# Reordered slots, a straight expert stage, and the Newton rounds of the rotary scale on POOL

## What is computed

```python
x = layernorm(x + ssm(x))              # state space layer, 64 states
x = layernorm(x + moe(x))              # three routed linears, 8 experts, top 2
x = layernorm(x + ssm2(x))             # second state space layer, 16 states
x = layernorm(x + transformer(x))      # 6 layers
```

```python
def attn_layer(x, Wqkv, qs, ks, Wo):       # 16 heads of 64
    q, k, v = split(x @ Wqkv)
    q, k = l2norm(q) * qs, l2norm(k) * ks
    q, k = rotary(q), rotary(k)            # cos and sin tables with a scale
    # queries in windows of 32 see their own and the previous window of keys, masked
    return softmax(8 * q @ k.T) @ v @ Wo

x = attn_layer(shift_tokens(x), ...) + x
x = (a * gelu(gate)) @ W2 + b2 + x         # a, gate = layernorm(shift_tokens(x)) @ W1 + b1
```

## Time and profile before

| | |
|---|---|
| median of 3 runs | 5227.65 us (5224.09 to 5231.3) |
| profiled execution | 5220.35 us |
| its span, first to last instruction | 5218.5 us |
| mean granted PE clock over the span | 0.924 |
| expert stage | 126 to 1033 us |
| transformer, its 96 full passes | some 1240 to 5100 us |

### The profile page before, as it was taken

How to read it: one execution, slowest core, us unless ns; L and a number is a source line. 1 busy time by engine, 2 the same in 40 slices (tenths; PEclk the granted TensorE clock), 3 DMA queues, 4 the chain that set the end, 5 groups by cost and what they waited for, 6 DMA issues and landing times.

```text
span 5218.5 us, 147460 instructions
## 1 busy us (share of the span) xinstructions
PE 4516.0 (87%) x64229; PEld 3255.0 (62%) x64613; DVE 3483.4 (67%) x7580; ACT 2311.9 (44%) x4138; POOL 2147.3 (41%) x1332
## 2 busy tenths in 40 slices
PE   4999899885888888888888888888888888888887
PEld 3666666563666666666666666666666666666665
DVE  5434343435777777777777777777777777778884
ACT  2111111122555555555555555555555555555553
POOL 0000000003555555555555555555555555555552
PEclk7999999997999999999999989999999999999997
DMA  1000000001111111111111111111111111111110
GB/s 70 1 1 0 0 0 0 9 1 43 29 33 30 33 41 39 33 31 32 41 39 33 33 29 44 40 33 30 36 43 38 30 30 33 45 39 32 32 33 24
DMA packets 70585, 152.25 MB, mean 29 GB/s; under 512 B 14523, under 2 KB 43078, under 8 KB 69574
## 3 DMA queue, kind: packets, MB, share of 16 engines
q1 hardware_dynamic: 69958, 143.09, 9.4%
HBM read 27.69 MB, written 2.10 MB: 6 GB/s over the span
## 4 chain that ended last, share of the span: by engine, by line
PE 44%; DVE 22%; ACT 5%; issue 5%; POOL 0%; DMA 0%; SPq 0%; DVEq 0%; POOLq 0%; ACTq 0%
PE pQ L1480 8%; PE pS L1464 7%; PE pO L1524 6%; PE pC L1580 5%; PE pO L1511 4%; ACT sq L1355 4%; PE pM L1546 4%; PE pM L1535 3%; PE pT L1511 3%; DVE E L1196 3%; DVE mx L1194 2%; DVE rot L1216 2%; DVE m L1220 2%; DVE ve L1254 2%; DVE n L1231 2%
## 5 line engine op out<-in xcount | busy, mean ns | idle before, releaser
L1138 POOL TENSOR_TENSOR rot<-rot,m 128x1024 f32<-128x1024 f32 x384 | 905.1, 2357 | 602.8 <-DVE m L1220 602.8
L1130 POOL TENSOR_TENSOR rot<-rot,rn 128x1024 f32<-128x1024 f32 x384 | 731.9, 1906 | 281.1 <-DVE rn L102 281.1
L1147 POOL TENSOR_TENSOR E<-E,rc 128x512 f32<-128x512 f32 x384 | 400.5, 1043 | 943.1 <-DVE rc L1206 943.0
L1346 ACT ACTIVATE E<-E 128x512 f32<-128x512 f32 x384 | 241.7, 629 | 1091.5 <-DVE E L1196 1091.5
L1511 PE MATMUL pO<-PT,V 64*64 64x32 f32 x12288 | 482.5, 232 | 199.6 <-ACT PT L1362 199.6
L1194 DVE TENSOR_REDUCE mx<-pS 128x8 f32<-128x512 f32 x384 | 264.2, 688 | 548.6 <-PE pS L1464 548.4
L1511 PEld LDWEIGHTS pO<-PT,V 64*64 64x64 f32 x12288 | 440.9, 149 | 284.2 <-issue 284.2
L1464 PE MATMUL pS<-kT,qT 64*32 64x64 f32 x24576 | 493.1, 238 | 87.1 <-issue 57.3
L1464 PEld LDWEIGHTS pS<-kT,qT 64*32 64x32 f32 x24576 | 424.0, 120 | 172.2 <-issue 172.1
L1216 DVE TENSOR_TENSOR rot<-pQ,tabl 128x1024 f32<-128x1024 f32 x384 | 469.5, 1223 | 54.0 <-ACT sq L1355 52.0
L1511 PE MATMUL pT<-PT,V 64*64 64x32 f32 x12288 | 484.6, 233 | 0.0
(11 more groups left out here) (221 smaller groups left out, 7932.3 us busy)
## 6 DMA issues: line engine op xcount, KB each, us to landing
V<-V SPq DMA_DIRECT2D x192, 384.0 KB, 3.5
xs<-XT SPq DMA_DIRECT2D x192, 64.0 KB, 2.9
V<-V SPq DMA_DIRECT2D x96, 128.0 KB, 3.3
ys<-XT SPq DMA_DIRECT2D x192, 64.0 KB, 2.0
wq<-in_wqkv SPq DMA_DIRECT2D x6, 512.0 KB, 4.0
wk<-in_wqkv SPq DMA_DIRECT2D x6, 512.0 KB, 4.0
wv<-in_wqkv SPq DMA_DIRECT2D x6, 512.0 KB, 3.9
wo<-in_wo SPq DMA_DIRECT2D x6, 512.0 KB, 4.0
```

The source lines that it names most:

```text
L1130: e.tensor_tensor(r, r, rn[n % 2][:, u * HEADS:(u + 1) * HEADS].unsqueeze(2).to_broadcast([P, HEADS, HD]), ALU.mult)\
L1138: e.tensor_tensor(rot[j % RING][:, :], rot[j % RING][:, :], m2[:, :, :].rearrange("p h d -> p (h d)"), ALU.add)\
L1147: e.tensor_tensor(ev, ev, rc[:, g, :].unsqueeze(2).to_broadcast([P, NW, KEYS]), ALU.mult).then_inc(g_no.sem, 1)
```

## The change

In the expert stage the loop goes and so does b_xst with POOL's copy: all 17 passes are written out, and PE and DVE read X itself. In the transformer the three Newton rounds move to POOL, ahead of unit_scale(R, 0), as four operations each; clamp and seed stay on DVE. All engines' lists get a new order: probs(Dn, 3) moves ahead, values(R, 0) into slot 0, and turn(R, 0) to that slot's end; values(R, 1) into slot 2; back becomes back(C) in slot 0 of the next pass. On DVE, statistics comes after rotate 0 and hidden after less_max 3 and rotate 3; POOL runs root after the first rotary_add; SP fetches the shifted half of V after the weights of the feed-forward and before ys, and the third weight at the end of the pass.

```diff
+def pool_rsqrt(eng, st, n, step, y, h, t):
+    def own(k):
+        eng.wait_ge(st.sem, st.at(step, n, 4 * ROUNDS - k))
+    for r in range(ROUNDS):
+        if r:
+            own(4 * r)
+        eng.tensor_tensor(t, y, y, ALU.mult).then_inc(st.sem, 1)
+        own(1 + 4 * r)
+        eng.tensor_tensor(t, t, h, ALU.mult).then_inc(st.sem, 1)
+        own(2 + 4 * r)
+        eng.tensor_scalar(t, t, 1.0, 1.5, ALU.mult, ALU.add).then_inc(st.sem, 1)
+        own(3 + 4 * r)
+        eng.tensor_tensor(y, y, t, ALU.mult).then_inc(st.sem, 1)
...
         def passes(run, eng):
-            run((0, 0), None)
-            run((1, 1), (0, 0))
-            with eng.Fori(0, (NSEQ - 2) // 2) as i:
-                for p in range(2):
-                    n = 2 * i + (2 + p)
-                    run((n, p), (n - 1, 1 - p))
-            run(None, (NSEQ - 1, 1))
+            for n in range(NSEQ + 1):
+                run((n, n % 2) if n < NSEQ else None, (n - 1, (n - 1) % 2) if n else None)
...
-                        e.wait_ge(gr.sem, gr.at("st", n))
                         if later(n):
                             e.wait_ge(ar.sem, ar.at("ctc", n - 1))
                         for t in range(T):
-                            m = e.transpose(pm[0][:, t * P:(t + 1) * P], xst[p][:, t * P:(t + 1) * P], ident[:, :])
+                            m = e.transpose(pm[0][:, t * P:(t + 1) * P], X[:, n, t, :], ident[:, :])
...
@@ SP @@
-                if R and starts(R):
-                    e.wait_ge(p_v.sem, p_v.at("b", 2 * R - 1))
-                    e.dma_start(wqkv[2][:, :], I["wqkv"][R // NSEQ, :, 2 * N:3 * N]).then_inc(wqkv_l[2], 16)
...
+                if R is not None:
+                    v, w = V[R % 2][:, :, 0, :], V[R % 2][:, :, 1, :]
+                    e.wait_ge(a_v.sem, a_v.at("b", 2 * R))
+                    e.dma_start(w[WIN:P, 0, :], v[0:P - WIN, 0, :]).then_inc(vs_l[R % 2], 16)
+                    e.dma_start(w[0:WIN, 1, :], v[P - WIN:P, 0, :]).then_inc(vs_l[R % 2], 16)
                 if Dn is not None:
                     fetch_ys(Dn)
...
                     e.wait_ge(a_v.sem, a_v.at("b", 2 * R + 1))
                     e.dma_start(w[WIN:P, 1, :], v[0:P - WIN, 1, :]).then_inc(vs_l[R % 2], 16)
+                    if starts(R + 1) and R + 1 < NP:
+                        e.dma_start(wqkv[2][:, :], I["wqkv"][(R + 1) // NSEQ, :, 2 * N:3 * N]).then_inc(wqkv_l[2], 16)
@@ POOL @@
                 if u == 0:
-                    e.wait_ge(v_nt.sem, v_nt.at("rs", n))
+                    e.wait_ge(v_nt.sem, v_nt.at("sd", n))
+                    pool_rsqrt(e, g_nt, n, "rs", rn[n % 2][:, :], rh[:, :], rt[:, :])
+                    e.wait_ge(g_nt.sem, g_nt.at("rs", n))
...
-                unit_scale(R, 0)
-                root(C)
-                by_sum(B, 0)
-                rotary_add(A, 0)
-                last_root(F)
-                for k in range(1, 4):
+                for k in range(4):
                     unit_scale(R, k)
                     by_sum(B, k)
                     rotary_add(A, k)
+                    if k == 0:
+                        root(C)
+                    if k == 1:
+                        last_root(F)
@@ DVE, roots @@
-                vector_rsqrt(e, v_nt, n, "rs", rn[n % 2][:, :], n2[:, :], rh[:, :], rt[:, :])
+                y = rn[n % 2][:, :].bitcast(I32)
+                e.wait_ge(v_nt.sem, v_nt.at("mn", n))
+                e.tensor_scalar(y, n2[:, :].bitcast(I32), 1, None, ALU.logical_shift_right).then_inc(v_nt.sem, 1)
+                if n:
+                    e.wait_ge(g_nt.sem, g_nt.at("rs", n - 1))
+                e.tensor_scalar(rh[:, :], n2[:, :], -0.5, None, ALU.mult).then_inc(v_nt.sem, 1)
+                e.wait_ge(v_nt.sem, v_nt.at("sh", n))
+                e.tensor_scalar(y, y, -1.0, MAGIC, ALU.mult, ALU.add).then_inc(v_nt.sem, 1)
```

More of the change, by code:

```diff
@@ L451, in _ @@
                 e.dma_start(dst, src).then_inc(loaded, 16)
[L453 to L462, removed]
         @block.vector
@@ L581, in r_lg @@
                         e.wait_ge(ar.sem, ar.at("xT", n))
[L582 removed]
+                        if n >= 2:
                             e.wait_ge(vm.sem, vm.at("lc", n - 2))
@@ L1317, in _ @@
                 squares(A, 1)
-                last_normal(F)
+                last_stats(F)
                 less_max(B, 2)
-                hidden(C, 0)
                 sums(B, 2)
@@ L1323, in _ @@
                 squares(A, 2)
+                last_normal(F)
                 less_max(B, 3)
+                hidden(C, 0)
+                sums(B, 3)
+                rotate(A, 3)
                 hidden(C, 1)
                 hidden(C, 2)
-                sums(B, 3)
-                rotate(A, 3)
-                ffn_add(C)
                 squares(A, 3)
                 roots(A)
+                ffn_add(C)
         @block.scalar
@@ L1403, in _ @@
             for A, R, B, Dn, C, F in passes():
+                probs(Dn, 3)
                 exponent(B, 0)
                 square(A, 0)
-                probs(Dn, 3)
+                heads_out(Dn, 3)
+                values(R, 0)
                 turned(R, 0)
-                heads_out(Dn, 3)
-                affine(C)
                 exponent(B, 1)
                 square(A, 1)
+                affine(C)
+                probs(B, 0)
+                turned(R, 1)
+                heads_out(B, 0)
+                probs(B, 1)
+                exponent(B, 2)
+                square(A, 2)
                 gelu(C, 0)
                 gelu(C, 1)
-                probs(B, 0)
-                turned(R, 1)
+                heads_out(B, 1)
+                turned(R, 2)
                 gelu(C, 2)
-                heads_out(B, 0)
-                exponent(B, 2)
-                square(A, 2)
-                probs(B, 1)
-                turned(R, 2)
-                heads_out(B, 1)
-                values(R, 0)
+                values(R, 1)
+                probs(B, 2)
                 exponent(B, 3)
                 square(A, 3)
-                probs(B, 2)
+                heads_out(B, 2)
                 turned(R, 3)
-                heads_out(B, 2)
-                values(R, 1)
         @block.tensor
@@ L1604, in _ @@
                 scores(B, 0)
+                probs(Dn, 3)
                 project(A, 0)
-                probs(Dn, 3)
+                back(C)
+                attend(Dn, 3)
+                values(R, 0)
                 turn(R, 0)
-                last(F)
-                attend(Dn, 3)
-                normed(C)
                 scores(B, 1)
                 project(A, 1)
+                normed(C)
+                combine(Dn)
+                probs(B, 0)
+                turn(R, 1)
                 hidden(C, 0)
-                probs(B, 0)
-                combine(Dn)
-                turn(R, 1)
+                attend(B, 0)
+                last(F)
+                scores(B, 2)
+                probs(B, 1)
+                project(A, 2)
+                attend(B, 1)
+                turn(R, 2)
                 hidden(C, 1)
-                attend(B, 0)
-                scores(B, 2)
-                project(A, 2)
+                values(R, 1)
+                scores(B, 3)
+                probs(B, 2)
+                project(A, 3)
                 hidden(C, 2)
-                probs(B, 1)
-                turn(R, 2)
-                attend(B, 1)
-                values(R, 0)
-                scores(B, 3)
-                project(A, 3)
-                contract(C)
-                probs(B, 2)
-                turn(R, 3)
-                attend(B, 2)
-                values(R, 1)
-                back(Dn)
+                attend(B, 2)
+                turn(R, 3)
+                contract(C)
 def layout(i):
```

29 lines of the change are left out of this document (12 added, 17 removed).

## The result

The changed kernel takes 5077.88 us (median of 3, 5071.0 to 5081.36) against 5227.65: ratio 0.9711, interval [0.9689, 0.9733]. The profiled execution took 5071.0 us, with a span of 5069.2 us. The forecast was 5066.

The account below looks back on a forecast made before the run. PE was taken to bound both stages, so its rests and low clock counted. From the profiled 5220 us, 75 (expert stage) and 79 (transformer) came off, giving 5066; own range 5010 to 5130, 8-in-10 range 4940 to 5205.

Parts of the forecast that it names:

- Expert stage, 75 us: Expert stage: 53 us of PE's wait plus 31 of slow clock, less 9 staying; ends 53 and 84.
- Newton on POOL, 0.35 each: Transformer slot 0: 12 dependent POOL operations at 0.35 us each, 4.2 us a pass; ends 1.3 and 8.4.
- the pow row: POOL's pow on two columns, 0.70 us: upper end per Newton operation, and the argument against leaving out the fixed part.
- Full-clock pass of 38.8: Transformer: one new pass walked at full clock takes 38.8 us, against 38.49 before.
- the port rule: Slot 0: POOL can block DVE's tensor_scalar through shared ports; ve could wait for the add, pass 39.2 instead of 38.8.
- The three rests of the walk: PE's rests in a new transformer pass: 2.1 us before contract, 1.4 before hidden 1, 0.55 before normed.
- Low clock, 0.7 us a pass: Transformer: low clock in a third to half of passes, 1.5 to 2.5 us each, 0.7 on average, giving 39.5.
- Transformer, 79 us: Transformer: passes fall from 40.33 to 39.5 us, times 95, a gain of 79 us.
- Sum, 154 us: Whole kernel: 75 us from the expert stage and 79 from the transformer, off 5220, giving 5066 us.
- The clock did not stay low in every pass: Rival, transformer: clock stays low in every pass, 40.96 us each, 5205 us in all; chance 0.15.
- POOL's operations kept under the 0.48: Rival, slot 0: POOL's chain bounds, a loss above 0.48 us per operation; at 0.70, 5465 us; chance 0.09.
- straight code did not come late: Rival, expert stage: straight code comes late, gaining only the rest or nothing, 5090 to 5145 us; chance 0.04.

Follow-up runs that it names:

- The filler: Changed kernel plus one thrown-away 512-column matmul per expert-stage sequence, between its last transposes and the third router's small matmuls: 5046.7 us, ratio 0.9642.
- fourth round: Changed kernel with a fourth Newton round on POOL, 4 more dependent operations: 5160.09 us, ratio 0.9863.
- The first experiment: Kernel before with only the straight expert stage (no loop, no b_xst), transformer untouched: 5153.44 us, ratio 0.9848.

## Why the prediction was right

- *Expert stage, 75 us:* 68, and 73 by the averages of all profiles. The rest of 3.8 us went whole and nothing came in its place; straight code cost nothing visible. The low clock was mis-sized twice. I had taken the first pair of sequences for the pattern (4.4 us of low clock for two), while over the whole stage it was 3.0 a sequence; and 1.5 a sequence stayed, where I had 0.6, so that they are 52.05 apart and not 50.4 to 51.5. The filler shows what it hangs on: with the stretch of transposes and 8-column matmuls broken up, every sequence takes 50.55.
- *Newton on POOL, 0.35 each:* 0.38. The two shapes gave the fixed part and the slope rightly; the pow row was no guide. That nothing covers the chain was right for a full-clock pass (fourth round: +1.5), not for a slow one (+0.5), where PE comes late anyway.
- *Full-clock pass of 38.8:* 39.05. The Newton rounds are 0.3 longer by the rows and the wait at hidden 1 is 0.24 shorter; no run takes the quarter apart. It is not the port rule, for which the prediction had named 39.2: in these passes ve took 0.28 and was not held by the add; it was held in the slow passes, where PE came late. The three rests of the walk stand in the waits, contract and normed within 0.1 us.
- *Low clock, 0.7 us a pass:* 0.6, but as two thirds of the passes at 1.0, not a third to a half at 1.5 to 2.5. The product was nearer than its two factors, and that is luck.
- *Transformer, 79 us:* 69, from two slips that partly cancel. The walked pass of 39.5 is one of the full pipeline, but was set against 40.33, a mean that takes in the three short passes of the filling. Without these three it is 40.58 before and 39.81 after. So like for like the forecast would have been (40.58 − 39.5) × 92 = 99 us, 20 more than stated, and the pass came out 0.3 longer than forecast, which is 28 us less.
- *Sum, 154 us:* 149. The two stages were 17 us too high in the forecast, and 12 us in the drain made up for it. The first experiment has nearly the same short drain with the old orders, so that part is for the most part luck of the clock: the terms were less good than the total.
- *Rivals:* The clock did not stay low in every pass, POOL's operations kept under the 0.48 from which they would have made a loss, and straight code did not come late. In the transformer the gain is that of the orders: the Newton rounds alone on POOL lose 43 us, and give 30 once the orders are there.

What the prediction did not ask is what these orders leave: 1.4 us of a full-clock pass and all of its low clock hung on one pair of instructions on ACT and one late pow.

## What to carry to other kernels

Where in-order queues of several engines are near balance, walk one period with start-to-start times: it finds the new rests and their length within 0.3 us, and also the cheap ones to move (a table load that waits behind a copy; a small operation at the end of another engine's chain). Treat every rest of PE as having two prices, its length and the low clock that may follow it; here splitting a rest, or filling it with matmuls that fit inside it, took away the second. Set a walked pass against passes of the same kind, not against a mean that takes in the filling of the pipeline. A term of luck such as the clock in a single drain should not be counted as a gain.

## What the hardware showed that I had not expected

- Filler matmuls inside a rest held the clock: 2 calls (1.7 us) in a rest of 2.0 took the transformer from a mean granted clock of 0.97 to 1.00 (1300 to 4700 us) and the kernel from 0.9711 to 0.9584.
- The same drain code took 119 and 108 us, at a granted clock of 0.78 and 0.88.
- The same two-column tensor_scalar on DVE took 0.28 or 1.67 us, by whether it came before or during a POOL add. The slow passes had the 1.67, so a wait seen in one slow pass does not explain the length of a fast one.
- A float32 matmul call with 512 columns ran as two matmuls, 0.43 us from start to start.
